# In an attention block, VectorE multiplies q and k by their norms ahead of the biases of heads 2 and 3, no longer behind them

## The reference, cut to what matters

```python
q = _rmsnorm((x @ Wq.T), q_norm_w)        # per head of 128
k = _rmsnorm((x @ Wk.T), k_norm_w)
scores = einsum(q, k) / sqrt(HD)
bias = where(rel > 0, NEG_INF, slopes * rel)
attn = softmax(scores + bias)
out = (attn @ v) @ Wo.T
```

## Time and profile before

| what | value |
|---|---|
| median of 3 runs | 817.59 us (813.06 to 818.42) |
| the profiled execution's own time | 813.07 us |
| its span, first to last instruction | 811.0 us |
| PE busy | 751.8 us (93%) |
| DVE busy | 580.2 us (72%) |
| ACT busy | 571.5 us (70%) |
| POOL busy | 364.1 us (45%) |
| granted TensorE clock, mean | 0.99 of full speed |

### The profile page before, as it was taken

One profiled execution on the slowest core, in us unless ns is written; L12 is line 12 of the kernel. 1 busy time (PEld: TensorE's weight loads), 2 busy tenths in 40 slices (PEclk: granted clock), 3 DMA queues, 4 the chain that ended last, 5 costly groups with the idle time before them and its releaser, 6 DMA issues.

```text
span 811.0 us, 14758 instructions
## 1 busy us (share of the span) xinstructions
PE 751.8 (93%) x4017; PEld 636.7 (79%) x4017; DVE 580.2 (72%) x1460; ACT 571.5 (70%) x1370; POOL 364.1 (45%) x281
## 2 busy tenths in 40 slices
PE   8888999999999999999999999989999999999757
PEld 7777878878787878878787888878788787878646
DVE  7847758676776868777785777778686768867443
ACT  4657777777767777687776777677776777678651
POOL 4312463345444453264444355244633554453374
PEclk9999999999999999999999999999999999999979
DMA  7025756365554647356454636437563655547341
GB/s 279 3 43 132 198 124 180 71 180 140 147 134 109 190 109 201 70 137 182 122 155 112 174 105 185 123 87 205 129 178 72 170 147 138 138 113 200 87 130 52
DMA packets 150675, 110.50 MB, mean 136 GB/s; under 512 B 44256, under 2 KB 141408, under 8 KB 150496
## 3 DMA queue, kind: packets, MB, share of 16 engines
q1 hardware_dynamic: 150624, 110.01, 51.2%
HBM read 66.97 MB, written 42.99 MB: 136 GB/s over the span
## 4 chain that ended last, share of the span: by engine, by line
PE 73%; DVE 9%; issue 8%; ACT 6%; POOL 1%; DMA 1%; SPq 1%; DVEq 0%; ACTq 0%
PE qkv_ps L1011 9%; PE qkv_ps L1012 9%; PE qkv_ps L1013 9%; PE out_ps L1011 6%; PE out_ps L1013 6%; PE out_ps L1012 6%; PE score_ps L1011 3%; PE turn_ps L1120 3%; PE score_ps L1013 3%; PE score_ps L1012 3%; PE mix_ps L1011 3%; PE mix_ps L1012 3%; PE mix_ps L1013 3%; DVE qk_norm L854 2%; ACT wo_hi L532 2%
## 5 line engine op out<-in xcount | busy, mean ns | idle before, releaser
L458 POOL TENSOR_TENSOR pt_lo<-x_sb,pt_hi 128x512 fp32r<-128x512 f32 x126 | 167.3, 1351 | 240.1 <-ACT pt_hi L610 240.1
L794 DVE CUSTOM_DVE_ANT_0 probs<-score_ps,cst,slope 128x128 f32<-128x128 f32 (+3 forms) x256 | 131.9, 548 | 159.8 <-PE score_ps L1013 124.3
L567 ACT ACTIVATE probs<-probs,neg_max 128x128 f32<-128x128 f32 (+3 forms) x256 | 141.7, 554 | 80.8 <-DVE neg_max L794 80.7
L1011 PE MATMUL qkv_ps<-w_hi,xt_hi 128*128 128x512 f32 (+1 forms) x512 | 179.9, 351 | 2.4 <-DVE xt_lo L743 1.4
L1012 PE MATMUL qkv_ps<-w_lo,xt_hi 128*128 128x512 f32 (+1 forms) x512 | 173.8, 339 | 0.0
L1013 PE MATMUL qkv_ps<-w_hi,xt_lo 128*128 128x512 f32 (+1 forms) x512 | 173.0, 338 | 0.0
L575 ACT ACTIVATE probs<-probs,recip 128x128 f32<-128x128 f32 (+3 forms) x256 | 129.9, 554 | 60.2 <-DVE recip L801 60.2
L450 POOL TENSOR_TENSOR inv_rms<-mean_sq,minus_half 128x5 f32<-128x5 f32 x64 | 75.0, 1172 | 110.2 <-DVE mean_sq L840 108.6
L1011 PEld LDWEIGHTS qkv_ps<-w_hi,xt_hi 128*128 128x128 f32 x512 | 97.1, 190 | 16.0 <-DVE xt_lo L743 1.7
L813 DVE STREAM_TRANSPOSE squared<-probs 128x256 f32<-128x256 f32 (+3 forms) x126 | 103.7, 824 | 3.1 <-ACT probs L575 3.1
L1013 PEld LDWEIGHTS qkv_ps<-w_hi,xt_lo 128*128 128x128 f32 x512 | 96.7, 189 | 11.6
(11 more groups left out here) (132 smaller groups left out, 1486.0 us busy)
## 6 DMA issues: line engine op xcount, KB each, us to landing
turning<-squared SPq DMA_DIRECT2D x120, 128.0 KB, 2.4
x_sb<-turning SPq DMA_DIRECT2D x30, 512.0 KB, 4.7
w_raw<-wqkv SPq DMA_DIRECT2D x32, 384.0 KB, 4.9
turning<-squared SPq DMA_DIRECT2D x128, 96.0 KB, 2.0
x_sb<-turning SPq DMA_DIRECT2D x32, 384.0 KB, 3.6
turning<-squared SPq DMA_DIRECT2D x128, 64.0 KB, 1.8
x_sb<-turning SPq DMA_DIRECT2D x32, 256.0 KB, 3.0
wo_raw<-wo SPq DMA_DIRECT2D x14, 512.0 KB, 5.7
```

The source lines that it names most:

```text
L458: nc.gpsimd.tensor_tensor(by_quad(pt_lo, j), moved_block(t, j), by_quad(pt_hi, j).bitcast(F32), ALU.subtract).then_inc(pt_lo_by_pool, 1)
L567: nc.scalar.activation(probs[:, h, 0:n], probs[:, h, 0:n], ACT.Exp, bias=neg_max[:, h:h + 1], scale=-1.0, accum_out=total[:, h:h + 1]).the ...
L794: nc.vector.tensor_tensor_reduce(probs[:, h, 0:n], score_ps[:, h % 2, 0:n], cst[:, C_DIST + SEQ - n:C_DIST + SEQ], slope[:, h:h + 1], HUGE ...
L1011: pe.matmul(out, a_hi, b_hi, start=start, stop=False)
```

## The change

In each of VectorE's slots, `normalize_qk` of block t+1 moves from behind the biases of heads 2 and 3 of block t to ahead of them, right behind the reciprocals of heads 0 and 1. No instruction is added or removed, and no other engine's list changes. The slots 0 and 1, written out by hand ahead of the others, stay as they are.

```diff
                 if here(t, left):
                     reciprocals(g, t, 0)
-                    bias(g, t, 2)
-                    bias(g, t, 3)
                 if here(t + 1, left):
                     normalize_qk(g, t + 1)
                 if here(t, left):
+                    bias(g, t, 2)
+                    bias(g, t, 3)
                     reciprocals(g, t, 2)
                     if not by_pe(t, left):
                         square_probs(g, t, 0)
```

## The result

| | before | changed |
|---|---|---|
| median (lowest to highest), us | 818.0 (813.06 to 820.31), 4 runs | 862.03 (860.41 to 863.09), 4 runs |
| profiled execution, us | 813.07 | 863.09 |
| its span, us | 811.0 | 861.3 |
| mean granted clock of TensorE in it | 0.992 | 0.958 |

The change makes the kernel slower: ratio 1.0545, 95% interval 1.0494 to 1.0596. That is 44 us by the medians, where 30 were forecast (848), and 4 us above the top of the range. The direction and most of the mechanism held; the size did not, and one step of the forecast, in slot 38, was wrong.

The account below looks back on a forecast made before the run. TensorE is busiest, with a VectorE/ScalarE chain to k_lo nearly as late. Six turns at 4.15 (24.9), first 3.6, end 5.1: +33.6 on 813.07 gives 846.7; median put at 848 us, range 828 to 858.

Parts of the forecast that it names:

- What bounds the kernel, and the sign: TensorE busiest, but k_lo without slack in slot 34: its 1.14 us wait moves to the scores, so the kernel gets slower.
- Slots 34 to 37: Later biases delay k_lo: TensorE +0.53 us at slot 35's start, +1.58 at 36's, +2.14 at 38's.
- Slot 38, the step that failed: inv_rms late through ScalarE and GpSimd: L1120 +1.80 us, late last w_lo puts TensorE's last chunk at +3.77.
- the exclusion of VectorE and GpSimd: In slot 36 mean_sq waits out GpSimd's third pt_lo; if not, some 1.1 us per turn, about 8 in total, are saved.
- `w_lo` itself: A new TensorE wait at L1011 for w_lo, about 2 us in each of seven turns.
- The signs: Profile signs: L852 wait some 60 us, L1120 wait below 25, k_lo wait above 25, turn 97.6 us with 89.5 busy.
- slot 39: TensorE's 0.61 us wait at L1120 goes and k_lo gives half of it back: +3.50 at slot 40.
- First group: Slots 2 to 9, without the loop's stall and slot 2's four copies: put at 3.6 us.
- The end: Slots 58 to 63: one more +0.53, slots like 39 and 40, 2.1 us in slot 62; together about 5.1 us.
- a turn costs 5: Top of the range: with more contention on GpSimd a turn costs 5 and the median sits high, 858 us.
- 0.09 faster: Rival: softmax not on the path, TensorE gets back its waits in slots 34, 38, 39: -26 us, 787; chance 0.09.
- 0.05 the same: Rival: k_lo late in some slots and earlier transposes in others cancel within 8 us; chance 0.05.

Follow-up runs that it names:

- e1: Changed kernel with L852 reading mean_sq in place of GpSimd's power (result not the reference's), plus a VectorE wait ahead of mean_sq: 805.58 us, ratio 0.9864.
- e9: Changed kernel with e3's wait and twelve unused matmuls on TensorE before each of two long waits (t = 6 and t = 3): 846.75 us, ratio 1.0383.
- e3: Changed kernel with GpSimd's w_lo held back until L852 is through, in slots with t = 6: 854.13 us, ratio 1.0456.
- e15: The changed kernel run and traced once more, nothing edited: 858.88 us, mean TensorE clock 0.984.
- e5: Changed kernel, but slots with t = 6 keep the old order: 847.21 us, ratio 1.0382.
- e8: Kernel before with the new order only in slots with t = 7: 815.81 us, ratio 1.0.
- e10: Kernel before with the new order for t = 7 and t = 6 (not slot 62), plus the edits of e3 and e4: 813.57 us, ratio 0.997.
- e2: Kernel before with the same edit as e1 (L852 reads mean_sq, one more VectorE wait): 811.79 us, ratio 0.9931.
- e12: Kernel before in its old VectorE order, with only ScalarE's w_hi and wo_hi copies moved: 815.23 us, ratio 0.9978.
- e13: Changed kernel with only the extra unused matmuls of e9, without the wait of e3: 861.64 us, ratio 1.0539.
- e14: The changed kernel run once more, nothing edited: 860.99 us, ratio 1.0535.
- e4: Changed kernel with ScalarE's last w_hi copy (t = 6) moved ahead of the exponentials of heads 2 and 3: 855.93 us, ratio 1.0473.

## Why the prediction was right, and where it was wrong

- **What bounds the kernel, and the sign: right.** `k_lo` had no slack in slot 34, TensorE's 1.14 us moved to the scores, and six turns grew by 5.6 us each. e1 confirms that the tie to GpSimd is the reason.
- **Slots 34 to 37: right to 0.15 us for TensorE** (table of shifts and the sentence behind it). In slot 35 head 2's bias starts 4.68 us after the first, where it was 2.69; in slot 36 `mean_sq` is held again, 1.15 us where the earlier trace rows had 0.96, as forecast. Slot 35 in the changed kernel:

```profile
469.52 0.75 DVE L794 CUSTOM_DVE_ANT_0 probs<-score_ps,cst,slope 128x512 f32<-128x512 f32 x1 [2.62 <-PE score_ps L1013]
...
473.46 0.82 DVE L854 TENSOR_TENSOR qk_norm<-qkv_ps,inv 128x640 f32<-128x640 f32 x1
474.20 0.74 DVE L794 CUSTOM_DVE_ANT_0 probs<-score_ps,cst,slope 128x512 f32<-128x512 f32 x1
```

- **Slot 38, the step that failed.** The forecast put L1120 at +1.80, the last chunk at +3.77; counted from the start of slot 34 they came at +3.14 and +5.14. Up to GpSimd's power it was right: `inv_rms` was done 53.4 us behind the start of slot 34, where 53.6 was forecast. But it took L852 at its usual 0.17 us behind `inv_rms` and named the exclusion of VectorE and GpSimd for `mean_sq` in slot 36 only. GpSimd's next `w_lo` starts right behind its power, and L852, with both its inputs in SBUF, ended only with it. Measured: 1.75 us, the slot adds 3.17 and not 1.63. Without it (e9) the slot adds 1.58 and a turn costs 3.9 where 4.15 were forecast. e3 alone does not show this, since there the clock hid three fifths. That e9's ratio of 1.0383 is 31 us, where 30 were forecast, is in part luck: its sum has 2.2 us before slot 2, where nothing was forecast, and less than forecast in the turns and at the end.
- **`w_lo` itself: right once TensorE's clock is full.** A wait of 2 us in each of seven turns was forecast; the first profile has 4.5 us in all, e15 has 13.7:

```profile
PE turn_ps L1120 <- DVE qk_norm L854: 30.9, 14, 7.8
PE score_ps L1011 <- DVE k_lo L826: 19.8, 9, 4.6
...
PE qkv_ps L1011 <- POOL w_lo L438: 13.7, 7, 2.0
PE score_ps L1107 <- DVE k_lo L826: 12.8, 15, 1.4
```

- **The signs.** VectorE's wait at L852, 72.5 us in 62 places: forecast about 60, right. The wait for `k_lo` above 25: 26.0, in e15 32.6, right. L1120 below 25: wrong, 29.4. It fell from 32 places to 10, but in the slots with t = 6 it grew from 1.28 to 2.44 each, and that is the same failed step: in e9 it is 20.9. Turn of 97.6 with 89.5 busy: 98.95 and 93.10; at full clock (e15) 99.06 and 90.09. In slot 39 the forecast had `k_lo` give back half of the 0.61 at L1120; it gave back nearly all (0.53).
- **First group: a small miss.** Slots 2 to 9 were forecast at 3.6; they cost 4.9 at full clock, 6.6 in the first profile. Most of the 1.3 over the forecast at full clock goes with L852 too, since e9 has 4.0.
- **The end.** The forecast had put 5.1 on slots 58 to 63 together. From slot 63 on alone the profiled executions differ by 4.0. This goes with TensorE's clock and not with the order. The changed kernel's first profile has a stretch at half clock there (the upper line, columns as above), in the kernel before the clock is full (the lower):

```profile
836.80:843.60 6.80, 6.18 (x15) 4.83 (x16) 1.22 (x2) 1.40 (x3) 6.26 (x5) 0.50 0.00 0
```

```profile
790.00:796.00 6.00, 5.91 (x29) 4.76 (x29) 0.99 (x2) 1.67 (x4) 5.92 (x6) 1.00 0.00 0
```

  Of the 17 profiles of this record, whichever order they have, six have no such stretch between the one that begins in slot 62 and the last 3 us, and take 31.1 to 31.5 us from slot 63 on (before, e3, e5, e8, e9, e10). Four have one of 3.4 us and take 32.7 to 33.9 (e2, e12, e13, e14), seven one of 6.8 us and take 34.2 to 35.1 (the changed kernel and e15 among them). The runs of the kernel before show the same 4 us: in one set of 13, the six with a mean clock of 0.991 to 0.994 average 813.7 us, the seven with 0.985 to 0.987 average 817.9. So of the 50 us between the two spans some 4 come from which execution was profiled; the medians' difference is 44. The 2.2 us of e9 before slot 2 are of the same sort: the five profiles with a stretch at half clock there (e4, e8, e9, e12, e13) reach slot 2 at 61.4 to 63.1 us, the others at 59.7 to 60.5.
- **The miss, added up by e15:** 0.1 before slot 2, 1.3 in slots 2 to 9, 8.1 in the six turns, 3.8 from slot 63 on, 0.9 less in slots 58 to 62: 12.4 us over the forecast's 33.6. The 8.1 has a shown cause, L852; it is 1.35 a turn, of 1.58 lost there. One more term was too small in the forecast's last step: it took 848 although its sum on the median of before would have been 851, so 3 us of the 14 between 848 and 862 were lost in choosing the base.
- **The range** put 858 at "a turn costs 5". The case was named, but too little of it was taken in: a turn cost 5.6. The rivals' own chances (0.09 faster, 0.05 the same) stand in the forecast's last line as 0.08 and 0.06.

**What stays open.** Why the same kernel runs some executions with fourteen stretches of 3.4 us at half clock in slots 2 to 58 and others with none, and why in e3 and e5 some slots have one and others of the same kind don't, after waits of the same length (1.96 in e3, 1.95 in e15), is not shown by any run. Nor is it shown what decides on the stretch in slot 63.

## What to carry to other kernels

When an edit puts a wait for another engine earlier, read what that engine does *next* and which memory the waiting instruction reads: work that lay in between may have covered a second, unnamed wait, and its only trace before was an instruction of 0.30 us where its kin took 0.17. Walk the turn slot by slot and follow the lateness through every list that stands in order; it came back through the weights, five slots on. A clock that is low while an engine has idle time to lose cost next to nothing here (0.6 us in six turns), and it started to cost when the thing that the engine was waiting for was mended, so test the two edits together as well as apart.

## What the runs showed of the chip that was not expected

- A VectorE product of 128x5 with both inputs in SBUF took 1.75 us, asked 0.06 us behind the start of a GpSimd instruction of 1.80 us, and ended with it. A `tensor_scalar` of 128x5 in front of it took 1.39 in the same way, ending with the `w_lo` before. Biases that read PSUM took their usual 0.61 over such an instruction.
- Stretches at half clock (0.50, 1.2 GHz) came to 13.7 us in the profiled execution of the kernel before, all in slots 61 to 63, and to 72.3 in that of the changed one: one of 3.4 us in each slot with t = 2 and t = 6 from slot 6 to slot 58, the rest at the end. The same kernel in e15 had 28.0, all at the end, with TensorE busy 21 us less (760.2 against 781.6), and was 4.4 us shorter, of which 1.8 lie in slots 2 to 9, 1.7 in slots 58 to 62 and 0.6 in the six turns.
